# Attention with future keys zeroed after the exponential instead of masked before it, in a kernel on one core

## The reference

```python
q, k, v = (qkv[0], qkv[1], qkv[2])            # 16 heads of 16 features
q = q * cos + _rotate_half(q) * sin
k = k * cos + _rotate_half(k) * sin
scores = jnp.einsum('bhqd,bhkd->bhqk', q, k) / math.sqrt(hd)
causal = jnp.triu(jnp.ones((S, S), dtype=bool), k=1)
scores = jnp.where(causal[None, None], -jnp.inf, scores)
attn = jax.nn.softmax(scores, axis=-1)
attn_out = jnp.einsum('bhqk,bhkd->bhqd', attn, v)
```

## Time and profile before

| | before |
|---|---|
| median of 3 runs | 1865.98 us |
| the three runs | 1863.89, 1865.98, 1879.54 us |
| profiled execution | 1862.59 us |
| its span, first to last instruction | 1860.8 us |
| TensorE matmul busy | 1734.3 us, 93% |
| VectorE busy | 993.0 us, 53% |
| ScalarE busy | 764.4 us, 41% |
| GpSimd busy | 660.6 us, 36% |
| mean granted TensorE clock | 0.970 |

### The profile page before, as it was taken

One profiled execution on the slowest core, in us unless ns is written; L12 is line 12 of the kernel. 1 busy time (PEld: TensorE's weight loads), 2 busy tenths in 40 slices (PEclk: granted clock), 3 DMA queues, 4 the chain that ended last, 5 costly groups with the idle time before them and its releaser, 6 DMA issues.

```text
span 1860.8 us, 38841 instructions
## 1 busy us (share of the span) xinstructions
PE 1734.3 (93%) x16212; PEld 1247.2 (67%) x16212; DVE 993.0 (53%) x2093; ACT 764.4 (41%) x1574; POOL 660.6 (36%) x832
## 2 busy tenths in 40 slices
PE   4866899999999999999999999999999999999888
PEld 2546645886468845887568855797458864788457
DVE  5775365636565365635655365744666365743531
ACT  4852345233552246233452245333462335423441
POOL 3242233523353332633353232733344232632110
PEclk8977999999999999999999999999999999999799
DMA  4001000000000000000000000000000000000000
GB/s 150 12 25 46 12 1 13 2 1 23 12 3 1 20 4 13 3 1 24 12 3 2 12 12 13 3 1 23 12 2 3 1 23 1 3 1 12 1 1 12
DMA packets 20236, 24.14 MB, mean 13 GB/s; under 512 B 960, under 2 KB 18912, under 8 KB 20064
## 3 DMA queue, kind: packets, MB, share of 16 engines
q1 hardware_dynamic: 19728, 20.62, 3.4%
q0 software_dynamic: 336, 1.05, 0.2%
HBM read 17.47 MB, written 4.19 MB: 12 GB/s over the span
## 4 chain that ended last, share of the span: by engine, by line
PE 74%; DVE 8%; ACT 5%; POOL 4%; issue 3%; POOLq 0%; DVEq 0%; ACTq 0%
PE ring L1473 17%; PE ring L1488 17%; PE ring L1449 5%; PE ring L1629 5%; PE ring L1459 5%; PE attn_out L1649 4%; PE ring L1587 3%; PE ring L1609 3%; PE ring L1612 2%; PE ring L1527 2%; PE ring L1632 2%; PE ring L1497 2%; PE ring L1441 2%; PE ring L1563 2%; POOL big L736 1%
## 5 line engine op out<-in xcount | busy, mean ns | idle before, releaser
L1234 DVE TENSOR_REDUCE maxes<-ring 128x2 f32<-128x1024 f32 (+7 forms) x294 | 198.1, 731 | 91.9 <-PE ring L1612 91.1
L684 POOL TENSOR_TENSOR rstd<-mean_var,eps_and_power 128x2 f32<-128x2 f32 x96 | 19.3, 201 | 496.2 <-DVE mean_var L1076 496.2
L1488 PE MATMUL ring<-w_down,big 128*128 128x256 f32 x768 | 172.4, 380 | 0.0
L736 POOL TENSOR_TENSOR big<-big,decay_blocks 128x256 f32<-128x256 f32 x192 | 142.7, 772 | 53.0 <-issue 45.2
L1488 PEld LDWEIGHTS ring<-w_down,big 128*128 128x128 f32 x768 | 144.5, 190 | 18.5
L707 POOL TENSOR_TENSOR mix<-mix,z_t 128x512 f32<-128x512 f32 x80 | 86.9, 1112 | 152.6 <-DVE mix L1123 152.6
L1167 DVE TENSOR_TENSOR big<-big,decay_blocks 128x256 f32<-128x256 f32 x192 | 135.1, 729 | 1.0
L1629 PE MATMUL ring<-big 32*128 32x512 f32 (+3 forms) x1024 | 123.3, 476 | 3.4 <-issue 1.7
L1473 PE MATMUL ring<-maxes,w_mlp 128*128 128x256 f32 x512 | 123.3, 397 | 0.0
L918 ACT ACTIVATE big<-ring,up_bias 128x256 f32<-128x256 f32 x192 | 80.5, 470 | 98.7 <-PE ring L1473 98.7
L1473 PE MATMUL ring<-maxes,w_up 128*128 128x256 f32 x512 | 115.9, 381 | 0.7 <-ACT maxes L860 0.7
(11 more groups left out here) (192 smaller groups left out, 3506.0 us busy)
## 6 DMA issues: line engine op xcount, KB each, us to landing
x_in<-in_x SPq DMA_DIRECT2D x8, 512.0 KB, 3.9
out<-x_z_xb SPq DMA_DIRECT2D x8, 512.0 KB, 2.9
delta<-in_x SPq DMA_DIRECT2D x7, 512.0 KB, 3.9
w_mlp<-in_wm SPq DMA_DIRECT2D x2, 1024.0 KB, 6.3
w_mlp<-in_w_exp_t SPq DMA_DIRECT2D x1, 1028.0 KB, 13.3
v_ones<-in_w_con SPq DMA_DIRECT2D x1, 1024.0 KB, 8.9
w_k<-in_wk SPq DMA_DIRECT2D x1, 512.0 KB, 6.2
w_r<-in_wr SPq DMA_DIRECT2D x1, 512.0 KB, 10.0
```

The lines of the kernel that those rows point to most:

```text
L736: nc.gpsimd.tensor_tensor(kv, kv, dv.unsqueeze(2).to_broadcast([P, T // (2 * s), s]), ALU.mult).then_inc(*one(kg_level))
L1234: nc.vector.tensor_reduce(maxes[:, t % 2, qt, 32 * gs[0] + row:32 * gs[-1] + row + 1:32], banks[:, first:last, lo:hi], AX_X, ALU.max).then ...
L1488: ins = mm(ps[:, a * D:(a + 1) * D], gelu(tag, m)[:, tok:tok + P], wd[:, m, :], start=(m == 0), stop=(m == NF - 1))
```

## The change

The mask matmuls of the E steps go. The exponential is now taken of unmasked scores, and a new step `hide t round` has VectorE overwrite the future keys in `pt` with zero, by a predicated copy whose mask is the same `future_t` read as integers and whose source is a column of zeros. Rounds a and c take one such instruction for the four heads together, round b two, since it holds two diagonal blocks. V waits for the copy of its round instead of for each head's exponential.

In the list, `hide a` stands behind the maxima of round a of the next group, `hide b` behind V a and ahead of the maxima of round b, `hide c` behind the maxima of round c. The second half of the value projection, `("v", 1, 1)`, moves from the end of group 2 to behind E a of group 3, and the second half of the gate projection, `("ga", 1)`, from behind V c of group 3 to ahead of it.

```diff
--- before.py
+++ after.py
@@ -127,17 +127,18 @@
                     [("proj", 1, 1, 0), ("proj", 1, 1, 1), ("rot", 1, 1, "all")],
                     [("k", 0, 0), ("k", 0, 1), ("k", 1, 0)], [("k", 1, 1)]],
                 1: [[("k", 2, 0), ("k", 2, 1)], mixed["C"], [], [("k", 3, 0), ("k", 3, 1)], mixed["D"]],
-                2: [[("v", 0, 0), ("v", 0, 1)], [], [], [("v", 1, 0)], [("v", 1, 1)]],
-                3: [[], [], [("ga", 0)], [], [("ga", 1)]]}[t]
+                2: [[("v", 0, 0), ("v", 0, 1)], [], [], [("v", 1, 0)], []],
+                3: [[("v", 1, 1)], [], [("ga", 0)], [("ga", 1)], []]}[t]
         o += [("E", t, "a")]
         o += [("divide", t - 1)] if t >= 1 else []
         o += [("S", t + 1, "a")] if ahead else []
-        o += fill[0] + [("E", t, "b")] + fill[1] + [("V", t, "a")]
+        o += [("hide", t, "a")] + fill[0] + [("E", t, "b")] + fill[1] + [("V", t, "a")]
+        o += [("hide", t, "b")]
         o += [("S", t + 1, "b")] if ahead else []
         o += [("roundq", 3, "all")] if t == 1 else []
         o += [("V", t, "b")] + fill[2] + [("E", t, "c")] if ahead else fill[2] + [("E", t, "c"), ("V", t, "b")]
         o += [("S", t + 1, "c")] if ahead else []
-        o += fill[3] + [("V", t, "c")]
+        o += [("hide", t, "c")] + fill[3] + [("V", t, "c")]
         if t == 0:
             o += [("fold", 1, 0, "all"), ("fold", 1, 1, "all"), ("roundk", 1, "all")] + halves(2)
             o += [("roundq", 2, "all")] + halves(3)
@@ -443,6 +444,7 @@
         maxs = sem("max_steps")
         qm_ready = sem("q_shifted", NG)
         pt_ready = sem("p_ready", NH * 3)
+        hidden_ready = sem("future_hidden", 3 * NG)
         pt_used = sem("p_used", 3 * NG)
         osum_ready = sem("osum_ready", NG)
         turned_ready = sem("sums_turned", NG)
@@ -1259,6 +1261,17 @@
                     nc.vector.tensor_tensor(osum[t], osum[t], inverse, ALU.mult).then_inc(*one(divided))
                     dve.wait_ge(*after(divided, NG))
                     nc.vector.tensor_tensor(osum[t - 1], osum[t - 1], osum[t], ALU.add).then_inc(*one(attn_ready))
+
+            def future_hidden(t, part):
+                dve.wait_ge(*after(pt_ready, exp_count(t, part, HG - 1)))
+                if b == 0 and t == 0 and part == "a":
+                    dve.wait_ge(*loaded(masks_in))
+                    dve.wait_ge(consts.h, N_CONSTS)
+                for at in (0, P) if part == "b" else (0,):
+                    ins = nc.vector.copy_predicated(pt[part][:, :, at:at + P], future_t.bitcast(U16).unsqueeze(1)
+                                                    .to_broadcast([P, HG, P]),
+                                                    zt[:, 0, 0:1].unsqueeze(1).to_broadcast([P, HG, P]))
+                ins.then_inc(*one(hidden_ready))
 
             def shift(t):
 
@@ -1397,6 +1410,8 @@
                     row_max(*at)
                 elif kind == "turn":
                     shift(*at)
+                elif kind == "hide":
+                    future_hidden(*at)
                 elif kind == "divide":
                     inverted(*at)
 
@@ -1618,7 +1633,6 @@
                     pe.wait_ge(*after(qp_ready, HALVES.index((t, 1, "all" if t else "high")) + 1))
                     pe.wait_ge(*after(qm_ready, t + 1))
                 parts = {"a": ((0, 0),), "b": ((1, P), (3, 0)), "c": ((2, 0),)}[rnd]
-                hi = 2 * P if rnd == "b" else P
                 ps = []
                 for i, (jt, at) in enumerate(parts):
                     n = T - jt * P
@@ -1626,11 +1640,10 @@
                         r = slice(32 * g, 32 * g + 32)
                         if i == 0:
                             ps.append(take(("E", t, rnd, g)))
-                        mm(ps[g][:, at:at + n], kp[r, t, jt * P:(jt + 1) * P], qp[r, t, jt * P:T],
-                           start=(i == 0), stop=False)
-                for g in range(HG):
-                    mm(ps[g][:, 0:hi], identb, future_t.unsqueeze(1).to_broadcast([P, hi // P, P]),
-                       start=False, stop=True).then_inc(*filled(("E", t, rnd, g)))
+                        ins = mm(ps[g][:, at:at + n], kp[r, t, jt * P:(jt + 1) * P], qp[r, t, jt * P:T],
+                                 start=True, stop=True)
+                        if i == len(parts) - 1:
+                            ins.then_inc(*filled(("E", t, rnd, g)))
 
             def pv(t, rnd):
 
@@ -1641,11 +1654,11 @@
                     if t == 0:
                         pe.wait_ge(*after(vaug_ready, 2))
                         pe.wait_ge(*after(clear_values, 1))
+                pe.wait_ge(*after(hidden_ready, used_count(t, rnd)))
                 for jt, lo in {"a": ((0, 0),), "b": ((1, P), (3, 0)), "c": ((2, 0),)}[rnd]:
                     n = T - jt * P
                     for g in range(HG):
                         m = NH // 2 * jt + HG * (t // 2) + g
-                        pe.wait_ge(*after(pt_ready, exp_count(t, rnd, g)))
                         ins = mm(obank[0][32 * g:32 * g + 32, jt * P:T], vaug[:, 48 * m + 16 * (t % 2):48 * m + 16 * (t % 2) + 32],
                                  pt[rnd][:, g, lo:lo + n], start=(jt == 0), stop=(jt == 2))
                 ins.then_inc(*one(pt_used))
```

## The result

| | before | after |
|---|---|---|
| median | 1865.51 us | 1958.04 us |
| range of the runs beside each other | 1863.89 to 1879.54 (4) | 1950.81 to 1959.57 (4) |
| profiled execution, its span | 1862.59, 1860.8 us | 1959.57, 1957.8 us |
| mean granted TensorE clock | 0.970 | 0.945 |

What follows compares the result with a forecast made beforehand. TensorE, 93% busy, was taken as the bound. Mask savings against copies and waits gave +3.5 us in each of 7 batches (24.5) and +6 in the last: about +30 on 1862.6, forecast 1893 us, range 1862 to 1912.

Steps and rivals of the forecast that it cites:

- groups 0 and 1: Middle batch: V b 0.8 us later and +0.65 carried on in group 0; +1.6 at the end of group 1.
- the last batch: Last batch's attention stage: +2 us in each of three groups, nothing in the fourth, +6 us in all.
- the whole prize: Removing 384 mask matmuls from TensorE: 4.7 us per batch, 37 us for 8 batches, if TensorE stays dense.
- 0.62 for one and 1.3 for a pair: VectorE's predicated copies: us per copy and per pair, bounds 0.33 and 0.75 for one; 83 us of VectorE time.
- Rival 3: TensorE's clock: waits bring one to two more half-speed stretches per batch, 12 to 24 us on top, 1905 to 1917; chance 0.15.
- the gate projection: Group 3: moved ahead of V c, it covers the copy of round c; no cost was put on it.
- a prize of 28 us: Mask matmuls priced by the skill's 56 ns per 128-column matmul: 9 us less to win than by the rows.
- group 2: Middle batch: V a +1.8, V b +2.3, V c +3.4 us; E a of the next group +3.35.
- E b of group 3: It waits for the bank freed by the moved value projection's evacuation, complete at 725.0; group 3 adds 0.65 us.
- V b of group 2: It waits for the pair of copies and starts at 713.5 against 711.25, +2.3 us.
- Rival 1: VectorE's copies cost half (0.33 us), 20 us less, 1873 us; half-price copies and small waits, chance 0.28.
- rival 2: TensorE's gain survives, copies falling into VectorE's idle time: 1825 us, or some 1843 with half lost; chance 0.12.

Runs made afterwards that it cites:

- narrow copies: The changed kernel with predicated copies of 8 columns per block instead of 128, same places and waits: 1913.07 us, ratio 1.025.
- in another order: The changed kernel with V b behind S c and its copies behind round b's maxima, plus 8, 4 and 4 unneeded matmuls ahead of S c: 1924.90 us.
- no masks, no copies: The kernel before without its mask matmuls, no copies, projections at their old places: 1855.44 us, ratio 0.995.
- no copies: The changed kernel without the predicated copies, V waiting for each head's exponential as before: 1862.40 us, ratio 0.997.
- copies aside: The changed kernel with its 16 copies per batch writing an unneeded tile, V waiting for the exponentials alone: 1922.59 us, ratio 1.030.

## Why the prediction was wrong

The direction was right, and so were the places of most waits; three terms of the sum were not. It took off 37 us for the masks and so put the copies and moves at 64 to 67 us. The runs show 10 and 103 (7 for the moves, 96 for the copies). Where in the middle batch the sum went wrong shows when both timelines are counted from the batch's first S matmul (650.21 before, 678.37 after):

| TensorE starts | later by, forecast (us) | later by, measured (us) |
|---|---|---|
| V b of group 0 | 0.8 | 2.2 |
| E a of group 1 | 0.65 | 3.5 |
| V b of group 1 | 1.6 | 6.1 |
| E a of group 2 | 1.6 | 9.6 |
| V c of group 2 | 3.4 | 11.5 |
| E a of group 3 | 3.35 | 11.5 |
| decay weights | 4.0 | 12.9 |

Groups 2 and 3 added 1.9 and 1.4 us, where 1.75 and 0.65 had been forecast. The miss lies in groups 0 and 1: 9.6 us instead of 1.6 (6.7 to 7.4 in the other five middle batches). There both the dearer pairs and the half-speed stretches stand. In the last batch, forecast at 6 us, the stage is 14 us longer (89.7 against 75.5).

1. **"for 8 batches 37 us. That is the whole prize, if TensorE stays dense."** It is 10 us. The price of the masks was right: put back beside the copies they add 35.8 us of busy time. The condition failed, and the earlier trace rows already spoke against it: S c of group 0 waited 0.22 us for the rotation. I used that row only for the copies' side of the sum. An engine that is 93% busy was taken for one whose input is always early; in truth chains on all three other engines followed within a few tenths of a microsecond, less than the masks ahead of them. In this term alone the sum was some 27 us too good, by 19 us of waits and, for the most part of the rest, a lower clock.
2. **"I take 0.62 for one and 1.3 for a pair".** Alone 0.72 and 1.33 to 1.35, so the bounds held. What they didn't cover is the neighbour: beside GpSimd's adds the pair takes 2.38 us in group 0 and 3.07 us in group 1. The adds were in the trace at these places; I priced the copy by its own kind's rows and never looked at what the other engine did there, though the copy's mask and source both lie in SBUF (those of the earlier trace rows have their source in PSUM, and none of the 96 takes over 0.47 us). Against the forecast's 1.3 that is 1.1 and 1.8 us more ahead of V b and of the maxima in groups 0 and 1: 21 us of copies in the whole kernel (63.5 against 42.8 us for the same copies where V b stands later). Short adds in groups 1 and 2 took 12 us off the copies, and some 13 us off the time. The 96 us of the copies are more than this: 60 of them are there when V doesn't wait for any copy: the maxima are queued behind, and the clock is lower.
3. **Rival 3, "One to two such stretches more per batch are 12 to 24 us on top", chance 0.15.** The forecast sum had waits of about 1 us and more in four or five places per batch and kept the clock as a chance beside it. Time at 1.2 GHz rose by about 103 us, so up to half of that, 51 us, is lost; TensorE's busy time, which should have fallen by some 37 us, rose by 1.6. So the rival was right in kind, and its price was too low. But its working read the earlier trace rows wrongly. E a of group 0 was spread over 2.35 us at a granted clock of 1.00, and the half-speed stretch came behind it, with TensorE busy for 3.92 of the 4.00 us ahead:

```profile
662.00:666.00 4.00, 3.92 (x22) 1.59 (x19) 2.79 (x5) 1.15 (x3) 3.11 (x3) 1.00 0.00 0
666.00:669.00 3.00, 3.00 (x8) 1.44 (x8) 2.36 (x2) 0.91 (x2) 1.13 (x2) 0.50 0.02 5
```

So a half-speed stretch can come without a long wait, and waits of 0.71 to 1.30 us can pass without one. The runs show that filling the waits of 2 to 3 us with work takes the stretches behind them away. They don't show a rule by which the number of stretches could have been forecast.

One cost was put at nothing without a reason: the gate projection, moved ahead of V c, no longer fills the time of the last division. The output projection then waits for it, 12.9 us in all instead of 4.0. This wait is there with and without copies, so it is part of what the moves cost.

The Trainium skill ("TensorE: Matmul & The Clock Gate", section "A second HAM failure mode: psum-queue depth-cycling") says that the clock swings between its levels when TensorE idles shortly and often between groups that cycle through PSUM banks. The runs with filled waits agree: two kernels that differ by 16 unneeded matmuls per batch took 1958.94 and 1924.90 us. The Trainium skill (same page, section "Wait — 56ns, not 53.3ns?") gives 56 ns for a 128-column matmul, by which the prediction's sum has a prize of 28 us. The measured 10 us is below both prices, as the price of a matmul didn't set it.

What held: group 2 (V a 1.30 and V c 1.05 us of idle time, the turn's 0.83 us no longer covered), E b of group 3 behind the evacuation (0.76), and moved projections that cost 7 to 10 us in the kernels without copies. Not so V b of group 2, which has no wait. Rival 1 (half-price copies) and rival 2 (faster) are out: the copies take 0.72 us or more, and no kernel with them came below 1913 us.

The account of the 93 us by experiments: the prize gives -10, the moved projections +7 (1855 to 1862), the copies +96. The copies' share divides into VectorE's queue, V's waits and the clock, which overlap: without V's waits 60 remain, with narrow copies 51, and with the gaps filled 62 (1924.90 against 1862.40, in another order). What the clock holds of it can be bounded by the profiled executions (us):

| | span | TensorE busy | idle | at 1.2 GHz |
|---|---|---|---|---|
| before | 1860.8 | 1734.3 | 126.5 | 112 |
| no masks, no copies | 1855.0 | 1709.7 | 145.3 | 148 |
| no copies | 1859.3 | 1700.7 | 158.6 | 130 |
| copies aside | 1922.2 | 1742.1 | 180.1 | 196 |
| after | 1957.8 | 1735.9 | 221.9 | 215 |

From the run without copies to after, idle time grows by 63 us and the same matmuls take 35 us longer; time at 1.2 GHz grows by 85 us, so at most some 43 us are lost to it. So about a third of the copies' price is matmuls that take longer, at the lower clock for the most part, and two thirds are waits (short waits inside a group of matmuls can hide in busy time). The 16 us (in this order) and 34 us (in the other) that unneeded matmuls gave back are net of what they cost.

## What to carry to other kernels

Before work is taken off the busiest engine, look at each wait of a few tenths of a microsecond ahead of it, and at each input that arrives just in time: the smallest slack there bounds the gain, not the busy time removed. Work handed to an engine with 47% of idle time can still cost most of its length, where that engine's next results are due: here 114 us of copies cost 96. The price of a copy must be looked up beside what the other vector engine does at that moment. On TensorE a forecast wait of 2 to 3 us, as here, may have two prices, its length and a half-speed stretch behind it; where the wait can't be removed, a few unneeded matmuls into a free bank can be the cheaper of the two. Count the change from place to place, too: the table above shows at once that the miss lies in two of four groups.

## What the runs showed of the hardware

- A predicated copy in SBUF (fp32 data, 16-bit mask) takes 0.72 us for 512 elements per partition and 0.19 us for 32. Beside GpSimd's tensor additions it is held up: pairs of 1.35 us take 2.38 us (one addition) and 3.07 us (three), and a pair of 32-element copies 2.09 us, about one addition for each. GpSimd loses too: three additions 3.64 us instead of 3.19.
- In two windows of 8 us TensorE was busy for 8.00 and 7.80 us at a granted clock of 0.60 and 0.69, behind waits of 2.15 and 2.88 us; with eight more matmuls in the first of these waits the clock was 1.00. In the kernel before, three microseconds at 0.50 came behind 4 us in which TensorE was busy for 3.92; in after, six waits of 0.71 to 1.30 us passed at 1.00.
- 128 unneeded matmuls of 512 columns made one kernel 34 us and another 16 us faster; 192 in a third, with a third of them where there was no gap, made no difference.
